# Who copies a scan's last column: 1,728 one-column copies move from VectorE to GpSimd in a four-layer convolution and scan network

## What is computed

```
# layer 1, per image                          # layer 3, forwards; then on the flipped sequence
deltaA = exp(delta[..., None] * A)            def step(h, inp):
dBu = delta[..., None] * B[:, :, None] * u        dA_l, dBu_l, C_l = inp
h = scan(h -> deltaA * h + dBu)  # along L        h = dA_l * h + dBu_l
y = einsum('bldn,bln->bld', h, C) + u * D         return h, einsum('bdn,bn->bd', h, C_l)
```

## Time and profile before

| what | value |
|---|---|
| time, median of 3 runs | 11139.65 us (11136.95 to 11142.12) |
| the profiled execution: its own time | 11141.17 us |
| its span, first to last instruction | 11139.1 us |
| granted TensorE clock, mean over the span | 0.972 |
| busy: PE / DVE / ACT / POOL | 94% / 79% / 71% / 52% |
| layer 1, scans from / to | 2992 to 6174 us |
| layer 3, scans from / to | 7239 to 11051 us |

### The profile page before, as it was taken

The page is one execution under the profiler, slowest core; times in us unless marked ns, Lnnn a source line. Parts: engine busy times, 40 slices in busy tenths (PEclk is TensorE's granted clock), DMA queues, the critical chain, the costliest instruction groups (busy, mean ns, idle before and its releaser), DMA issues. The chain is left out here.

```text
span 11139.1 us, 128149 instructions
## 1 busy us (share of the span) xinstructions
PE 10416.8 (94%) x41860; PEld 5841.7 (52%) x41860; DVE 8778.3 (79%) x8226; ACT 7929.4 (71%) x14477; POOL 5817.0 (52%) x2580
## 2 busy tenths in 40 slices
PE   9999999999899999999999999999999999899896
PEld 6767767677544444444444445444444444444442
DVE  6848848668599999999999212188888888998997
ACT  5636636556488888888888554588888887777775
POOL 0000000000288788887888100088888888888885
PEclk9999989989899999999999999999999999999998
DMA  1000000000145445444545000044444444454455
GB/s 39 0 0 0 0 1 0 0 0 0 51 168 172 170 171 170 170 172 168 171 170 176 27 8 15 28 154 158 158 162 158 156 164 159 160 169 159 160 169 205
DMA packets 325678, 1207.41 MB, mean 108 GB/s; under 512 B 36624, under 2 KB 36752, under 8 KB 321552
## 3 DMA queue, kind: packets, MB, share of 16 engines
q1 hardware_dynamic: 325232, 1201.95, 31.7%
HBM read 1145.18 MB, written 56.62 MB: 108 GB/s over the span
## 5 line engine op out<-in xcount | busy, mean ns | idle before, releaser
L1786 POOL TENSOR_TENSOR l_ring<-l_ring 128x1024 f32<-128x1024 f32 x1024 | 2429.0, 2394 | 609.6 <-DVE l_ring L1868 608.2
L907 POOL TENSOR_TENSOR l_hc<-l_h,l_hc 128x1024 f32<-128x1024 f32 x1024 | 2412.8, 2378 | 613.2 <-DVE l_h L1018 612.6
L1868 DVE TENSOR_TENSOR_SCAN l_ring<-l_ring,l_carry,l_ps 128x1024 f32<-128x1024 f32 x960 | 2200.5, 2332 | 7.1 <-PE l_ps L1496 5.9
L1506 PE MATMUL l_ps<-l_ring,w_sb 128*128 128x512 f32 x4096 | 1983.5, 607 | 86.7 <-POOL l_ring L1786 55.1
L663 PE MATMUL l_ps<-l_hc,w_sb 128*128 128x512 f32 x4096 | 1946.1, 597 | 32.5 <-POOL l_hc L907 26.9
L1018 DVE TENSOR_TENSOR_SCAN l_h<-l_decay,l_carry,l_ps 128x1024 f32<-128x1024 f32 x768 | 1759.7, 2333 | 3.5
L114 POOL COPY l_qm<-l_q 128x128 f32 x128 | 82.4, 646 | 2733.3 <-PE l_ps L175 2335.0
L798 ACT ACTIVATE l_decay<-l_delta,w_sb 128x1024 f32<-128x1024 f32 x1024 | 1161.7, 1139 | 289.0 <-DVE l_h L1018 287.7
L1663 ACT ACTIVATE l_ring<-l_delta,w_sb 128x1024 f32<-128x1024 f32 x1024 | 1164.5, 1139 | 190.6 <-DVE l_ring L1868 189.5
L1676 ACT ACTIVATE l_xt<-l_duT,l_BT 128x128 f32<-128x128 f32 x4096 | 1246.0, 388 | 0.0
L811 ACT ACTIVATE l_xt<-l_duT,l_BT 128x128 f32<-128x128 f32 x4096 | 1246.0, 387 | 0.0
(11 more groups left out here) (229 smaller groups left out, 14741.4 us busy)
## 6 DMA issues: line engine op xcount, KB each, us to landing
l_hc<-l_rows_dram SPq DMA_DIRECT2D x1024, 512.0 KB, 3.7
l_ring<-l_rows_dram SPq DMA_DIRECT2D x1024, 512.0 KB, 3.7
l_gate_dram<-l_gate SPq DMA_DIRECT2D x32, 512.0 KB, 5.3
l_recon_dram<-l_recon SPq DMA_DIRECT2D x32, 512.0 KB, 5.3
l_gate<-l_gate_dram SPq DMA_DIRECT2D x32, 512.0 KB, 5.4
l_xw<-x_dram SPq DMA_DIRECT2D x30, 513.5 KB, 5.1
x_dram<-x SPq DMA_DIRECT2D x16, 512.0 KB, 2.6
l_loaded<-l_recon_dram SPq DMA_DIRECT2D x16, 512.0 KB, 5.1
```

Of the source, the lines that this page charges most:

```text
L907: nc.gpsimd.tensor_tensor(hc[:, unit % CS, :], h[:, unit % HS, :], hc[:, unit % CS, :], ALU.mult).then_inc(hc_done, 1)
L1506: ins = nc.tensor.matmul(y_sum[:, half(j)], ident, hc[:, unit % CS, half(j)], start=q == 0, stop=q == S3 - 1)
L1786: nc.gpsimd.tensor_tensor(hc[:, unit % CS, :], h[:, unit % HS, :], hc[:, unit % CS, :], ALU.mult).then_inc(hc_done, 1)
L1868: nc.vector.tensor_tensor_scan(h[:, unit % HS, order], decay[:, unit % DS, order], x_now[:, order], before, ALU.mult, ALU.add).then_inc(sc ...
```

## The change

`keep` goes from VectorE's list, with its wait on `scan_done`. `product` on GpSimd now waits for the scan first, copies the column if the chunk has a successor, counts it in `kept`, then waits for the row of C and multiplies. The waits of `scan` stay as they are, but what they count is now done by another engine. The number of copies and what they copy are the same.

```diff
--- before.py
+++ after.py
@@ -902,8 +902,11 @@
                 nc.gpsimd.tensor_tensor(yg[:], yg[:], cg[:], ALU.add).then_inc(yg_ready, 1)
 
             def product(unit):
+                K, q = divmod(unit, S1)
+                pool.wait_ge(scan_done, unit + 1)
+                if K % NC < NC - 1:
+                    nc.gpsimd.tensor_copy(carry[:, q:q + 1], h[:, unit % HS, CH - 1:CH]).then_inc(kept, 1)
                 pool.wait_ge(c_in[unit % CS], 16 * (unit // CS) + 16)
-                pool.wait_ge(scan_done, unit + 1)
                 nc.gpsimd.tensor_tensor(hc[:, unit % CS, :], h[:, unit % HS, :], hc[:, unit % CS, :],
                                         ALU.mult).then_inc(hc_done, 1)
 
@@ -1017,11 +1020,6 @@
                 before = carry[:, q:q + 1] if K % NC else zero[:]
                 nc.vector.tensor_tensor_scan(h[:, unit % HS, :], decay[:, unit % DS, :], odd_in if odd else even_in,
                                              before, ALU.mult, ALU.add).then_inc(scan_done, 1)
-
-            def keep(unit):
-                q = unit % S1
-                dve.wait_ge(scan_done, unit + 1)
-                nc.vector.tensor_copy(carry[:, q:q + 1], h[:, unit % HS, CH - 1:CH]).then_inc(kept, 1)
 
             dve.wait_ge(weights_in, 32)
             nc.vector.memset(zero[:], 0.0)
@@ -1055,9 +1053,6 @@
                         add_y(K - 1, 1 - p)
                     if P + 1 < NCH * PAIRS:
                         even_input(P + 1, p if k + 1 < PAIRS else 1 - p)
-                    if K % NC < NC - 1:
-                        keep(2 * P)
-                        keep(2 * P + 1)
                     if k == 1 and K:
                         gate_conv(K - 1, 1)
                     if k == 21:
@@ -1781,8 +1776,14 @@
                     nc.gpsimd.tensor_tensor(yg[:, S % 3, :], yg[:, S % 3, :], gate[:, e, :], ALU.mult).then_inc(gated_ready, 1)
 
                 def product(unit):
+                    S, q = divmod(unit, S3)
+                    K, e = divmod(S, TI)
+                    pool.wait_ge(scan_done, unit + 1)
+                    if K % NCH < NCH - 1:
+                        at = CH - 1 if forward(K) else 0
+                        nc.gpsimd.tensor_copy(carry[:, e * S3 + q:e * S3 + q + 1],
+                                              h[:, unit % HS, at:at + 1]).then_inc(kept, 1)
                     pool.wait_ge(c_in[unit % CS], 16 * (unit // CS) + 16)
-                    pool.wait_ge(scan_done, unit + 1)
                     nc.gpsimd.tensor_tensor(hc[:, unit % CS, :], h[:, unit % HS, :], hc[:, unit % CS, :],
                                             ALU.mult).then_inc(hc_done, 1)
 
@@ -1868,13 +1869,6 @@
                     nc.vector.tensor_tensor_scan(h[:, unit % HS, order], decay[:, unit % DS, order], x_now[:, order],
                                                  before, ALU.mult, ALU.add).then_inc(scan_done, 1)
 
-                def keep(unit):
-                    S, q = divmod(unit, S3)
-                    K, e = divmod(S, TI)
-                    at = CH - 1 if forward(K) else 0
-                    dve.wait_ge(scan_done, unit + 1)
-                    nc.vector.tensor_copy(carry[:, e * S3 + q:e * S3 + q + 1], h[:, unit % HS, at:at + 1]).then_inc(kept, 1)
-
                 def pieces(S, r):
                     K, e = divmod(S, TI)
                     if e == 1 and K + 1 < NK:
@@ -1911,9 +1905,6 @@
                         add_y(S - 1)
                     if P + 1 < NS * PAIRS:
                         even_input(P + 1)
-                    if S // TI % NCH < NCH - 1:
-                        keep(2 * P)
-                        keep(2 * P + 1)
                     pieces(S, r)
                 add_y(NS - 1)
                 for j in range(2):
```

## The result

| | before | changed |
|---|---|---|
| median of the runs on the same chip (6 each) | 11140.89 us | 11186.33 us (11182.40 to 11188.26) |
| ratio to before, 95% interval | | 1.0041 [1.0028, 1.0054] |
| the profiled execution: time, span | 11141.17, 11139.1 us | 11188.26, 11186.2 us |
| TensorE clock, mean over the span | 0.972 | 0.972 |
| layer 1, first scan to the end of the last | 3181.3 us | 3197.1 us |

The change costs 45 us, where 100 were forecast. In the profiled executions layer 1 takes 15.8 us more and layer 3 28.3; the other layers differ by 3 us. The direction was right and the size more than twice too large.

A forecast was written before the change was run, and what follows sets the result against it. VectorE was taken to bound layer 1, GpSimd's list from pair 1 to `input_rate` to set pair 5 in layer 3. Terms -6 + 72 + 14 + 20 = +100 us gave 11240 us, range 11168 to 11331 us.

The forecast's parts named there:

- What bounds layer 3: Layer 3: GpSimd's list from pair 1 to `input_rate` sets the time of pair 5 in every sweep.
- from 147 us to about 147 + 72 = 219: Layer 3: expected rise of TensorE's wait for GpSimd's `input_rate` in the new profile.
- 480 copies x 0.15 = +72 us: Layer 3: GpSimd's copies of pairs 1 to 4, 8 a sweep in 60 sweeps, cost 0.15 us each.
- The estimate of 0.20 us: GpSimd: size-independent time of an instruction, from the skill's 4497 ns; by it the sum would be +129 us.
- 0.04 us that back-to-back products are said to gain: GpSimd: products standing back to back gain only 0.04 of their 2.35 us; said against the nearly free copy.
- The clock ... 12 x 1.7 = +20 us: Layer 3: longer TensorE idle before `turn_du` brings 12 more sweeps a lowered clock, 1.7 us each.
- Both its ends, 0 and 41: Layer 3: lower and upper ends, in us, given for the clock term of +20 us.
- Layer 1, "-6 + 14": Layer 1: -6 us from 4 gaining pieces a chunk, +14 us from four SBUF pieces ending two copies later.
- VectorE's new wait for `kept` at 0: Layer 3: `scan` now waits through `kept` for GpSimd, later by one copy only; costed at 0.
- the dear copy (0.29 us): Rival, GpSimd: a copy costs 0.29 us, giving +191 us, 11331 us; chance 0.18.
- the one at 0.03 us: Rival, GpSimd: the copy is nearly free at 0.03 us, giving +11 us, 11151 us; chance 0.12.
- VectorE's saving of 18 us in layer 3: Rival: pair 5 set by VectorE's pieces, layer 3 gains 18 us, -24 with layer 1, 11116 us; chance 0.04.

The follow-up runs named there:

- two fills: Two unused TensorE products in front of `turn_du` in every layer 3 sweep: kernel before 11067.95 us (0.9933), changed kernel 11129.02 us (0.9989).
- early `input_rate`: `input_rate` moved right behind `soft_sum` in GpSimd's layer 3 list: kernel before 11071.16 us (0.994), changed kernel 11155.61 us (1.0015).
- kernel without copies: Kernel before with none of the 1728 copies made by any engine, every chunk's scan starting from zeros: 11145.9 us (1.0004).

## Why the prediction was right or wrong

- **What bounds layer 3** was right. The half of the copies on GpSimd's stretch from pair 1 to `input_rate` carries the cost, the other half none, and with twice the copies `input_rate` is late by twice as much. The stretch measured 32.79 us where 33.0 was said, and a product starts 0.14 us behind its copy where 0.15 was. Too narrow was the point at which the path ends: TensorE meets GpSimd's lateness in `add_state` as well, so the rise of TensorE's wait for `input_rate` "from 147 us to about 147 + 72 = 219" failed (162.5), while the two waits together rose by 44 us, near the 48 by which the sweeps grew.
- **"480 copies x 0.15 = +72 us"** measured 48. The price is most of it: `input_rate` came 0.89 us later in an odd sweep, 0.11 us a copy and not 0.15, which makes 480 x 0.11 = 53. The estimate of 0.20 us that the prediction set beside its own was further off. (The 0.04 us that back-to-back products are said to gain does not follow from the 4.69 us beside it: 2 x 2.35 - 4.69 is 0.01, and from start to start it is 2.35 - 2.32 = 0.03.) The rest is that sweeps did not grow alike: by 0.47, 0.86, 1.19 and 0.62 us (even and odd forwards, even and odd backwards), where `input_rate` came 0.49, 0.88, 1.20 and 0.88 later. Why the even backward sweeps lose more and the odd backward ones less was not traced. In the even forward sweeps `input_rate` came only 0.48 us later, since `soft_round` now gets in at a copy and takes 1.02 us where it took 2.92, so that GpSimd's idle time in front of `soft_low` goes (VectorE's line first, then GpSimd's):

```profile
7522.18 1.02 DVE L1824 TENSOR_SCALAR l_z<-l_z 128x1024 f32<-128x1024 f32 x1
...
7520.29 2.36 POOL L1787 TENSOR_TENSOR l_ring<-l_ring 128x1024 f32<-128x1024 f32 x1
7522.59 0.66 POOL L1784 COPY l_carry<-l_ring 128x1 f32<-128x1 f32 x1
7523.20 2.35 POOL L1787 TENSOR_TENSOR l_ring<-l_ring 128x1024 f32<-128x1024 f32 x1
7525.51 2.37 POOL L1755 TENSOR_TENSOR l_z<-l_z 128x1024 f32<-128x1024 f32 x1
```

- **"The clock ... 12 x 1.7 = +20 us"** is the step that failed, with 39 of the 55 us between forecast and result. It had the wrong sign: the time at the lower clock fell by 37 us and gave 19 back. Its premise failed first: in an odd sweep the idle stretch did not grow from 2.2 to 3.4 us but to 2.4, since TensorE's work in front of it moved along (2.17 to 2.84 in most even forward sweeps, 2.73 to 2.85 in even backward ones). That the count of lowered stretches rises with the length of the idle time was an assumption. The two fills show that these stretches follow from the idle time. The count rose with its length in the kernels with the early `input_rate`, and fell as it grew here. Both its ends, 0 and 41, excluded what happened, for the text had bounded it from above and below by the number of sweeps that could join, and none that could leave.
- **Layer 1, "-6 + 14"** measured +16, just over the 15 us within which layer 1 was to stay. Six pairs gained, not four (-9 us in 12 chunks). The pairs whose pieces have all tiles in SBUF became longer as said, by 0.2 us rather than 0.30 (+10 us). At three of the four this fits two copies of 0.12 us less the 0.06 that these pairs lost without copies too. At pair 12, `split_rest` starts 1.12 us behind `even_input` and took 2.82 us for 2.53:

```profile
4077.64 1.20 DVE L1008 TENSOR_TENSOR l_ps<-l_du,l_ps 128x1024 f32<-128x1024 f32 x1
4078.76 2.82 DVE L961 SCALAR_TENSOR_TENSOR l_rest<-l_part,w_sb,l_rest 96x1024 f32<-96x1024 bf16 x1
4081.50 2.33 DVE L1021 TENSOR_TENSOR_SCAN l_h<-l_decay,l_carry,l_ps 128x1024 f32<-128x1024 f32 x1
```

  Missing was the place where GpSimd has no room although it has 612 us in the layer: pair 4, and with it pair 0, 1.4 us a chunk or 17 us in 12. The three together make 18 by medians, for the 15.8 of the layer.
- **VectorE's new wait for `kept` at 0** was right: `even_input` to scan stayed within 0.01 of its 1.24 us (4021.41 to 4022.66 in layer 1), and the list of waits shows no wait of VectorE for GpSimd's copies.
- The sum of what was measured: 48 (copies in layer 3) - 19 (clock) + 16 (layer 1) = 45 us, which is what the medians show. Against the forecast's terms these are misses of -24, -39 and +8 us; the last one hid part of the other two. Of the rivals, the dear copy (0.29 us) and the one at 0.03 us are excluded by the timeline, and VectorE's saving of 18 us in layer 3 by the kernel without copies.

Open is why the changed kernel has fewer stretches at the lower clock. In three of the four kinds of sweep of the kernel before, the idle times with and without a drop behind them have the same length (2.17 us in odd forward sweeps, 2.73 and 2.18 in even and odd backward ones). In even forward sweeps a drop follows 3 of 6 idle times of 2.72 us and 1 of the other 10. So length plays a part at most, and something else in the sequence decides.

## What to carry to other kernels

When work moves to an engine with room on average, list the places at which another engine waits for it, and count what stands ahead of each; a copy of 0.11 us costs nothing at one pair and its full time in 60 sweeps at another. Add up all the waits of one engine for another over its lines before and after: a single line can move to its neighbour, as the early `input_rate` showed, where one wait fell from 151 us to 4 and the sum only from 206 to 175. And first ask what the removed work is worth by leaving it out altogether: here that run said zero in the medians and at most 13 us in the traces, so a move can pay only where GpSimd is waiting anyway. And compare such small gains with the clock taken out, since it gave or took 5 to 77 us in these kernels.

## What the runs showed of the hardware

- A GpSimd copy of one column lasts longer in the trace than it costs in a row of work. All copies of layer 3 (ns: least, median, most):

```profile
L1784 POOL COPY l_carry<-l_ring x960: 173/185/1208, 7261.8 to 10994.6; 128x1 f32<-128x1 f32 x192
```

  Each is recorded with 185 ns, but adds 0.10 to 0.12 us to a row of products, and 0.12 again for the second of two copies in a row.
- A VectorE operation with all tiles in SBUF that waits behind GpSimd's products gets in at a boundary made by a small GpSimd instruction: `soft_round` took 1.02 us instead of 2.92, and the copy 0.66 instead of 0.19. Even 8 columns are held so: `newton`'s first operation, 128x8, took a median of 1264 ns, 786 before, and 0.17 us at least. VectorE's own one-column copies, from SBUF to SBUF too, were not held: at 8150.01 two took 0.21 us while a product ran. The Trainium skill, SBUF — State Buffer, section "SBUF: two separate sides", says of the port that VectorE and GpSimd share that whichever starts first has it for its whole instruction and the other "fully blocks"; for VectorE it means operations in a two-port mode or with two inputs in SBUF. The trace, which does not tell the mode, agrees that it blocks, and shows more. In the odd sweep of the earlier trace rows `soft_round` came while the first of two products ran (8149.24, 4.68 us for both) and sat through the second as well:

```profile
8150.14 4.34 DVE L1823 TENSOR_SCALAR l_z<-l_z 128x1024 f32<-128x1024 f32 x1
```

- Two matmuls that compute nothing, put into TensorE's idle stretch, made the kernel before 0.7% faster: by 72 us, with 1.00 for the granted clock of layer 3 in place of 0.98. Its 2.2 to 2.7 us of idle time in every sweep cost nothing by themselves: sweeps that kept the clock are as long without the fill (57.75 us, even forwards) as with it (57.70). What they cost is the clock behind them.
